# Moving two LayerNorms of an attention and mixture-of-experts kernel to other stages

## The reference, cut to what matters

```python
x1 = _layernorm(x + attn(x, x, x, causal), ln1)            # L0 self-attention
x2 = _layernorm(x1 + attn(x1, ctx, ctx), ln2)              # L0 cross-attention
x3 = _layernorm(x2 + moe(x2), ln3)                         # 8 experts, top 2, gelu
# L1: pre-norm cross-attention and MLP
q  = layer_norm(x3, l1_ln1)
kv = layer_norm(ctx, l1_ln1)                               # the context's LayerNorm
x4 = x3 + attn(q, kv, kv)
out = x4 + gelu(layer_norm(x4, l1_ln2) @ w1 + b1) @ w2 + b2   # l1_ln2: the last closing LayerNorm
```

## Time and profile before

| what | value |
|---|---|
| median of three runs | 1596.96 us (1593.52 to 1598.0) |
| profiled execution, its own time | 1599.19 us |
| its span | 1597.5 us |
| busy time, PE / DVE / ACT / POOL | 1262.5 (79%) / 961.3 (60%) / 988.5 (62%) / 916.6 us (57%) |
| mean TensorE clock granted | 0.885 of full speed |
| HBM traffic | 95.45 MB read, 50.86 MB written, 92 GB/s |
| `at_` stage, about | 0 to 580 us |
| router | 580 to 685 us |
| expert tiles | 685 to 960 us |
| combine | 961 to 1172 us |
| second block's attention | 1172 to 1472 us |
| final MLP | 1472 to 1597 us |

### The profile page before, as it was taken

The page is one execution under the profiler, slowest core; times in us unless marked ns, Lnnn a source line. Parts: engine busy times, 40 slices in busy tenths (PEclk is TensorE's granted clock), DMA queues, the critical chain, the costliest instruction groups (busy, mean ns, idle before and its releaser), DMA issues. The chain is left out here.

```text
span 1597.5 us, 60681 instructions
## 1 busy us (share of the span) xinstructions
PE 1262.5 (79%) x23128; PEld 1057.0 (66%) x23128; DVE 961.3 (60%) x2185; ACT 988.5 (62%) x2032; POOL 916.6 (57%) x1424
## 2 busy tenths in 40 slices
PE   4999999999999843879999990212149999993998
PEld 2778787778878743779999990111127787872676
DVE  4777777778787605945555553666537788881001
ACT  2778787778888600956666661545437788882333
POOL 2466675666767510079999866777324676662111
PEclk9999999999999955889999995555559999997999
DMA  3223333233332134012222223565422233322343
GB/s 100 89 88 99 96 92 103 85 94 105 92 105 89 52 122 129 0 47 70 67 68 69 67 61 103 154 171 157 128 87 87 86 99 104 106 62 62 91 118 93
DMA packets 169852, 147.65 MB, mean 92 GB/s; under 512 B 19104, under 2 KB 132256, under 8 KB 169760
## 3 DMA queue, kind: packets, MB, share of 16 engines
q1 hardware_dynamic: 161312, 129.11, 26.7%
q0 software_dynamic: 8448, 17.32, 4.6%
HBM read 95.45 MB, written 50.86 MB: 92 GB/s over the span
## 5 line engine op out<-in xcount | busy, mean ns | idle before, releaser
L741 DVE TENSOR_REDUCE at_mx<-at_ps_s 128x16 f32<-128x1024 f32 x128 | 156.0, 1219 | 107.7 <-PE at_ps_s L490 61.0
L678 ACT ACTIVATE at_pt<-at_ps_t 128x1024 f32<-128x1024 f32 x128 | 130.6, 1020 | 54.5 <-PE at_ps_t L504 53.8
L1338 POOL DMA_INDIRECT ex_xg<-x,ex_ti x136 | 148.1, 1089 | 23.3 <-issue 21.7
L671 ACT ACTIVATE at_pr<-at_dd 128x1024 f32<-128x1024 f32 x128 | 135.1, 1056 | 35.2 <-DVE at_dd L749 35.2
L1398 ACT ACTIVATE ex_hg<-ex_ps_h,ex_wt 128x128 f32<-128x128 f32 x544 | 154.8, 374 | 1.2 <-PE ex_ps_y L1367 1.2
L749 DVE TENSOR_TENSOR at_dd<-at_ps_s,at_mx 128x1024 f32<-128x1024 f32 x128 | 153.5, 1201 | 0.1
L1548 POOL DMA_INDIRECT cb_yg<-rows,cb_sl x128 | 124.9, 976 | 46.5 <-issue 44.9
L1419 DVE COPY ex_wt<-experts 128x1156 f32 x136 | 104.8, 772 | 75.4 <-DVE ex_y L1425 72.9
L1358 PE MATMUL ex_ps_h<-ex_xt,ex_wt 128*128 128x128 f32 x1088 | 147.6, 279 | 0.0
L504 PE MATMUL at_ps_t<-ident,at_pr 128*128 128x128 f32 x1024 | 140.2, 280 | 5.0 <-issue 3.1
L1367 PE MATMUL ex_ps_y<-ex_wt,ex_hg 128*128 128x128 f32 x1088 | 143.8, 275 | 0.3 <-ACT ex_hg L1398 0.3
(11 more groups left out here) (236 smaller groups left out, 3310.5 us busy)
## 6 DMA issues: line engine op xcount, KB each, us to landing
rows<-ex_y SPq DMA_DIRECT2D x136, 64.0 KB
x<-at_ln_out SPq DMA_DIRECT2D x32, 256.0 KB, 3.1
at_kx<-in_xt SPq DMA_DIRECT2D x16, 256.0 KB, 2.8
at_qx<-in_xt SPq DMA_DIRECT2D x16, 256.0 KB, 2.8
at_vin<-in_xt SPq DMA_DIRECT2D x16, 256.0 KB, 2.8
at_xr<-in_x SPq DMA_DIRECT2D x16, 256.0 KB, 3.1
x1t<-at_xt SPq DMA_DIRECT2D x16, 256.0 KB, 3.2
at_kx<-in_ctxt SPq DMA_DIRECT2D x16, 256.0 KB, 2.8
```

The lines of the kernel that those rows point to most:

```text
L671: act.activation(pr[:, p], dd[:, p], ACT.Exp, scale=SCALE).then_inc(p_ready, 1)
L678: act.activation(pt[:, 2 * h + p], ps_t[:, :, :, :], ACT.Copy).then_inc(pt_ready, 1)
L741: dve.tensor_reduce(mx[:, p], ps_s[:, :, 4 * p:4 * p + 4, :], AX.X, ALU.max).then_inc(mx_ready, 1)
L1338: pool.indirect_dma_start(out=xg[:, s, :], out_offset=None, in_=x_src, in_offset=bass.IndirectOffsetOnAxis(ap=ti[:, s:s + 1], axis=0)).the ...
```

## The change

Two LayerNorms change stage.

- **The context's.** It leaves `combine_phase` (12 statistics per group become 8, one ScalarE scaling of 4 tiles, 4 transposes and one ScalarE copy go, with a load and a store). It enters `expert_phase`, one group of 512 context tokens in each pass of 8 expert tiles. The load is issued by SyncE at tile 2 of pass q, VectorE takes statistics at tiles 4 and 5 (`context_statistics`). GpSimd computes the root (`context_root`) after its gather of tile 1 of pass q+2. VectorE scales at tile 1 of pass q+1 (`scale_context`), TensorE transposes at tile 2, VectorE copies at tile 3 (`copy_context`), and SyncE stores at tile 5. To free a PSUM bank for the transpose, `ex_ps_h` goes from four buffers to two, so `up` of tile i+2 now waits for gelu of tile i. `over_tiles` unrolls two passes at its start instead of one.
- **The last closing one.** The attention stage `l1_` no longer computes it (`closing` is false when the layer stores y), and `x4t` is gone. `mlp_phase` loads x4 three groups ahead, takes statistics on VectorE, the root on GpSimd, scales on ScalarE between its gelus, transposes on TensorE and copies on VectorE. Gain and shift are folded once into `w1g` and `b1s`.

```diff
 def attention_phase(nc, c, tag, layers):
+    closing = not layers[0].store_y
...
-                    if beyond(g, 1):
+                    if closing and beyond(g, 1):
                         pe.wait_ge(vx_ready, g + 1)
                         turn_x(a.shift(-2))
...
-                        if beyond(g, 1):
+                        if closing and beyond(g, 1):
                             pe.wait_ge(xt_ready, g - 1)
                         else:
-                            pe.wait_ge(vx_ready, 2)
+                            pe.wait_ge(vx_ready, g + 1)
                         project_out(a.shift(-1))
...
-                    if a.shift(-2).exists():
+                    if closing and a.shift(-2).exists():
                         ln.pool_rstd(pool, a.shift(-2))
...
 def mlp_phase
                 def step(g, u, k, first, last):          # TensorE
                     for f in range(FC):
                         if f < FC - 1:
-                            up(g, u, k, f + 1)
+                            up(g, u, f + 1)
                         elif not last:
-                            up(g + 1, 1 - u, k if u == 0 else k + 1, 0)
+                            up(g + 1, 1 - u, 0)
                         down(g, u, k, f)
-                up(0, 0, 0, 0)
-                over_groups(pe, step)
+                        if f == 0 and not last:
+                            turn(g + 1, 1 - u)
+                pe.wait_ge(ld, 48)
+                for f in range(FC):
+                    mm = pe.matmul(ps_b[:, f:f + 1], w1[:, P * f:P * f + P], c.col["l1_ln2_b"][:, 0:1], start=True,
+                                   stop=True)
+                mm.then_inc(fold_ready, 1)
+                turn(0, 0)
+                pe.wait_ge(w1_ready, 1)
+                up(0, 0, 0)
+                over_groups(pe, step, 1, 2)
...
+                    for f in range(3):                   # ScalarE
+                        gelu(g, f)
+                    if ahead:
+                        scale(g + 2, u, 0, 2)
+                    gelu(g, 3)
+                    if ahead:
+                        scale(g + 2, u, 2, 4)
...
+                def step(g, u, k, first, last):          # VectorE
+                    if before(g, NG - 2):
+                        moments(g + 2, u, k + 2)
+                    if not first:
+                        add(g - 1, 1 - u, k - 1 + u)
+                    if not last:
+                        copy_z(g + 1, 1 - u)
+                moments(0, 0, 1)
+                moments(1, 1, 1)
+                dve.wait_ge(fold_ready, 1)
+                dve.tensor_tensor(b1s[:, :], b1[:, :], ps_b[:, :], ALU.add)
+                dve.tensor_scalar(w1g[:, :], w1[:, :], c.col["l1_ln2_g"][:, 0:1], None, ALU.mult).then_inc(w1_ready, 1)
+                copy_z(0, 0)
...
-def expert_phase(nc, c, r, tag, x_src, out_rows):
+def expert_phase(nc, c, r, tag, x_src, out_rows, ctx_src, ct_out):
...
-        ps_h = [n.ps(f"ps_h{i}", [P, FC, P]) for i in range(HB)]
+        ps_h = [n.ps(f"ps_h{i}", [P, FC, P]) for i in range(2)]
+        ps_c = n.ps("ps_c", [P, GT])
...
+                def context_root(q):
+                    pool.wait_ge(cmv_ready, q + 1)
+                    pool.tensor_tensor(cvar[:, :], cmv[:, :, 1], c.eps[:, 0:GP], ALU.add).then_inc(cvar_ready, 1)
+                    pool.wait_ge(cvar_ready, q + 1)
+                    pool.tensor_tensor(crstd[:, :], cvar[:, :], c.minus_half[:, 0:GP], ALU.pow).then_inc(crstd_ready, 1)
+
+                def with_context(i, s, q, first, last):
+                    step(i, s, q, first, last)
+                    if s == 1 and beyond(q, 1):
+                        context_root(q - 2)
                 copy_number(0, 0)
-                over_tiles(pool, step)
+                over_tiles(pool, with_context)
+                context_root(NG - 1)
...
-                    if beyond(i, HB - 1):
-                        pe.wait_ge(hg_ready, i - HB + 1)
+                    if beyond(i, 1):
+                        pe.wait_ge(hg_ready, i - 1)
...
                     down(i, s)
+                    if s == 2 and not first:
+                        turn_context(q - 1)
...
+                def context_statistics(q, half):
+                    if half == 0:
+                        dve.wait_ge(in_c, 16 * q + 16)
+                    for t in (2 * half, 2 * half + 1):
+                        ins = dve.bn_stats(cstats[:, t, :], cx[:, t, :])
+                    if half == 0:
+                        return
+                    ins.then_inc(cstats_ready, 1)
+                    dve.wait_ge(cstats_ready, q + 1)
+                    dve.memset(ctick[:, :], 0.0)
+                    for t in range(GP):
+                        ins = dve.bn_aggr(cmv[:, t, :], cstats[:, t, :])
+                    ins.then_inc(cmv_ready, 1)
+
+                def scale_context(q):
+                    dve.wait_ge(crstd_ready, q + 1)
+                    for t in range(GP):
+                        ins = dve.tensor_scalar(zc[:, t, :], cx[:, t, :], cmv[:, t, 0:1], crstd[:, t:t + 1],
+                                                ALU.subtract, ALU.mult)
+                    ins.then_inc(zc_ready, 1)
...
                     if inside(s, last, 3):
                         weights(i + 3, (s + 3) % TU)
+                    if s == 1 and not first:
+                        scale_context(q - 1)
+                    if s == 3 and not first:
+                        copy_context(q - 1)
+                    if s in (4, 5) and not last:
+                        context_statistics(q, s - 4)
...
 def combine_phase                                        # ScalarE
-                    if not first and before(g, NG + 1):
-                        act.wait_ge(in_c[1 - u], 16 * (kp + 1))
-                        if beyond(g, 2):
-                            act.wait_ge(tc_ready, g - 2)
-                        scale(zc[:, 1 - u], cx[:, 1 - u], 1 - u, CTX).then_inc(zc_ready, 1)
```

More of the change, by code:

```diff
@@ new lines, in gelu @@
+                def gelu(g, f):
+                    m = g * FC + f
+                    act.wait_ge(h_ready, m + 1)
+                    if beyond(m, 1):
+                        act.wait_ge(used, m - 1)
+                    act.activation(hid[:, f % 2, :], ps_h[f % 2][:, :], ACT.Gelu,
+                                   bias=b1s[:, f:f + 1]).then_inc(hid_ready, 1)
+                def step(g, u, k, first, last):
+                    ahead = before(g, NG - 2)
+                    for f in range(3):
[5 more added lines that the diff above has]
+                        scale(g + 2, u, 2, 4)
@@ L1274, in mlp_phase, with step @@
+                def step(g, u, k, first, last):
+                    if before(g, NG - 2):
+                        root(g + 2, u)
+                    if not last:
+                        add_bias(g + 1, 1 - u, k + u + 1)
+                root(0, 0)
+                root(1, 1)
+                add_bias(0, 0, 1)
+                over_groups(pool, step, 1, 2)
         n.clear()
 def over_tiles(eng, step):
-    for s in range(TU):
-        step(s, s, 0, True, False)
-    with eng.Fori(1, NT // TU - 1) as q:
+    for q in range(2):
+        for s in range(TU):
+            step(q * TU + s, s, q, q == 0, False)
@@ L1283, in over_tiles @@
+    with eng.Fori(2, NT // TU - 1) as q:
         for s in range(TU):
@@ L1316, in _, with load_context, store_context @@
             def _(sp):
+                def load_context(q):
+                    if beyond(q, 0):
+                        sp.wait_ge(zc_ready, q)
+                    sp.dma_start(cx[:, :, :], ctx_src.rearrange("(g t p) d -> g p t d", t=GP, p=P)[
+                        bass.ds(q, 1)].rearrange("o p t d -> p (o t) d")).then_inc(in_c, 16)
+                def store_context(q):
+                    sp.wait_ge(zct_ready, q + 1)
+                    sp.dma_start(ct_out[:, bass.ts(q, GT)], zct[:, :]).then_inc(zc_stored, 16)
                 def step(i, s, q, first, last):
+                    if s == 2 and not last:
+                        load_context(q)
+                    if s == 5 and not first:
+                        store_context(q - 1)
                     sp.wait_ge(y_ready, i + 1)
@@ L1320, in _ @@
                 over_tiles(sp, step)
+                sp.wait_ge(zc_stored, 16 * NG)
                 for s in range(TU):
@@ L1369, in down, with turn_context @@
                     mm.then_inc(down_ready, 1)
+                def turn_context(q):
+                    pe.wait_ge(zc_ready, q + 1)
+                    for t in range(GP):
+                        tr = pe.transpose(ps_c[:, P * t:P * t + P], zc[:, t, :], c.ident[:, :])
+                    tr.then_inc(tc_ready, 1)
                 def step(i, s, q, first, last):
@@ L1588, in step @@
                         tr.then_inc(t4_ready, 1)
-                    if not first and before(g, NG + 1):
-                        pe.wait_ge(zc_ready, g)
-                        if beyond(g, 2):
```

(6 more changed lines are left out.)

281 lines of the change are left out of this document (173 added, 108 removed).

## The result

The changed kernel takes 1610.56 us in the median of four runs (1609.36 to 1612.61), the kernel before 1597.48 us in the same comparison: a ratio of 1.0086, with a 95% interval of 1.0063 to 1.0109, or +13 us. The profiled execution took 1612.61 us with a span of 1610.9 us, 13.4 us more than before.

A forecast was written before the change was run, and what follows sets the result against it. TensorE and VectorE's weights copies, with GpSimd tied to them, bound the expert stage; gathers pace combine. Sum: 31 - 4 - 7.4 - 6.0 + 7.4 = +21 us, 1620 us (1618 on the median's level), range 1609 to 1627.

The forecast's parts named there:

- Expert stage, +31 forecast: Expert stage: added transposes, VectorE insertions and waits for the root cost +31 us, bounds 7.8 to 38.
- Every insertion between a copy and the next `ex_y` delays the next copy by its length less 0.28 us.: Expert stage, VectorE: only 0.28 us is covered, the next `up` delayed equally; a pass without waits loses 1.14 us.
- A wait of 0.9 to 1.4 us in each pass.: Expert stage: VectorE's scaling waits for GpSimd's root in each pass, taken as 1.0 us; a pass loses 1.95 us.
- Rival A: Expert stage: GpSimd's root is in time, no VectorE waits after pass 1; whole +8 us, 1605; chance 0.19 including some B.
- Rival B: Expert stage: the pow blocks weights copies, up to 14.7 us above Rival A, 1605 to 1619; chance split with forecast.
- Rival C: Expert stage: weights copy off the path, insertions fit VectorE's idle time; stage +7.8, whole -2 us, 1595; chance 0.11.
- Rival E: Expert stage: two buffers make TensorE wait for gelu in each tile, 14 us more, up to 1632; chance 0.03.
- the two buffers "at nothing": Expert stage: two `ex_ps_h` buffers in place of four cost nothing, as gelu ends 0.28 us before `up`.
- Combine, -4 forecast: Combine: last steps' chain shortens by 3.4 us, last gathers land 0.6 us earlier; sum -4, bounds 0 and -12.
- rival D: Combine: weights copy off the path and gathers' pace quickens, 0.5 us a round, 8 us; time 1587; chance 0.09.
- Second attention, -7.4 forecast: Second attention: 14 groups lose 0.49 us of transposes, -6.9 us, and relieved other engines give -0.5 us.
- Boundary, -6.0 forecast: Between attention and MLP: MLP starts 9.4 us earlier, its first `up` comes 3.4 us later after start; net -6.0 us.

The follow-up runs named there:

- padded kernels: Kernel before with two or four extra VectorE operations in step 1 of each pass, which nobody waits for: 1.0018 and 1.0028 of before.
- e8_after: The changed kernel itself, unaltered, compared again with the kernel before: 1.0079 of before.
- e3_root: Changed kernel with the context's root three gathers earlier in GpSimd's queue, behind tile 6: 1.0078 of before.
- e7_root7: Changed kernel with the context's root two gathers earlier in GpSimd's queue, behind tile 7: 1.0068 of before.
- e10_noroot: Changed kernel without the context's root, scaling by the variance instead: 1.0017 of before, +2.7 us.
- e11_closing: Kernel before with only the closing LayerNorm's move, repeated on another chip: 0.9996 of before.
- e5_pad2: Kernel before with two extra 128x128 VectorE operations in step 1 of each pass, which nobody waits for: 1.0018 of before, +2.9 us.
- e6_pad4: Kernel before with four extra 128x128 VectorE operations in step 1 of each pass, which nobody waits for: 1.0028 of before, +4.5 us.
- e1_closing: Kernel before with only the closing LayerNorm's move (attention and MLP of the kernel after), first comparison: 0.9953 of before.

## Why the prediction was right in direction and where its steps were off

The forecast was +21 us (1620 on the profiled level), the measurement +13 us, inside the forecast's own range but near its lower edge. Direction and stage were right. So was the mechanism, a GpSimd queue tied to VectorE's copies and a root that comes too late, except that it strikes in half of the passes. The largest term was too large by some 9 us. Part of the agreement is luck: combine came out 2.7 us better than forecast, attention and boundary together 5.8 us worse, and inside the expert stage errors of both signs cancel.

- **Expert stage, +31 forecast, +22 measured.** Two terms of it were mis-sized. The sign "gaps on TensorE before `ex_ps_h` released by `ex_wt`" came true in small: 0.20 to 0.36 us in 14 passes, behind the statistics. The gaps after a wait for the root end on `ex_zc` and `ex_xt`.
  - *"Every insertion between a copy and the next `ex_y` delays the next copy by its length less 0.28 us."* The cover is larger. The 0.56 us between `ex_y` and the copy was taken as fixed. It shrinks as `ex_y` gets later, down to 0.14 us, and 0.28 + 0.42 = 0.70 us would be covered. The two padded kernels show 0.48 (0.60 less 0.12) and 0.78 us (1.11 less 0.33). A pass without the wait costs 0.65 us and not 1.14. If the transposes cost the 0.49 us of the forecast, 0.16 are left for VectorE's work; in the MLP, where TensorE has no gaps either, the same four cost 0.43. A second error went the other way: the four scalings take 1.12 us, taken as 0.6 and outside the bounds of 0.5 to 0.87.
  - *"A wait of 0.9 to 1.4 us in each pass."* The wait is 1.2 us, but in every second pass (8 of 16). The forecast had GpSimd tied to one gather for each copy. The trace after shows it tied except just after a wait, where it makes several gathers 1.48 us apart (802.74, 804.22, 805.70) and gains enough for one pass. So the passes 2 to 15 cost 1.2 us on average, not 1.95: 14 x 0.73 = 10 us of the error. Another 2.4 us are the second pass, 0.65 us in place of 3.1. There the forecast's 2.3 us of waiting did come true in `e8_after` (2.26 us, a pass of 17.97), and was hidden in the profiled run by its late start. The half clock and the late third `up` at the stage's start, and 0.9 us at its end, bring back 3.5 us, which the sum did not have.
- **Rival A, the root in time.** It holds in every second pass. The thought behind it, that 13.1 us of own work fit in a pass of 15.2, fails: `e3_root` and `e7_root7` put the root earlier and gained nothing that can be told, and without the root the stage lost 8.3 us of its 18.5. GpSimd makes use of its spare time only where VectorE isn't copying.
- **Rival B, the root blocks a weights copy.** It doesn't. The copies' mean went from 772 to 783 ns, 1.5 us over the stage, and the long ones, up to 1.00 us, start beside the end of a gather and not beside a pow. The kernel before has eleven of 0.86 us at such places, and `e10_noroot`, which has no root, has two of 1.00. The Trainium skill ("SBUF — State Buffer", Who interferes with whom) lets whichever of the two engines starts first block the other for its whole instruction. The trace agrees where the copy is first (a root addition of 0.75 us at 798.26, beside the copy from 798.20, against 0.20 for such an addition in the MLP). For the reverse it differs. This copy starts 0.44 us into a pow and takes its usual 0.76 us, while the pow takes 1.24 in place of 1.04:

```profile
960.12 1.24 POOL L1499 TENSOR_TENSOR ex_crstd<-ex_cvar,minus_half 128x4 f32<-128x4 f32 x1
...
960.56 0.76 DVE L1592 COPY ex_wt<-experts 128x1156 f32 x1 [0.56 <-DVE ex_y L1598]
```

  In `e3_root` a copy that starts 0.02 us behind a pow of 1.04 us takes 0.79. Spans on GpSimd are rough, but the copy's length isn't that of a blocked one.
- **Rival C, the copy isn't on the path.** Refuted by the padded kernels: work that nobody waits for costs 0.12 and 0.33 us a pass. It was nearer than its 0.11 suggested: with 16 x 0.49 = 7.8 us for the transposes, VectorE's insertions without the root cost 2.4 of the 10.2 us. This is an estimate, for no run had the transposes alone.
- **Rival E and the two buffers "at nothing".** Right in the steady stage. The start was not looked at: a wait of 0.7 us there.
- **Combine, -4 forecast, -6.7 measured.** The LayerNorm steps of the end gave 3.2 us (3.4 forecast), the earlier landing of the last gathers 3.4 (0.6 forecast) in this pair of traces. The 6.1 us of before are high, though: `e11_closing` has 4.7 with the same combine, so 1.4 us of it are that one trace's, and the earlier landing is worth 2.0. Gathers stay 1.25 us apart and take 178.5 us together in both kernels, and rival D falls.
- **Second attention, -7.4 forecast, -3.8 measured.** A group takes 15.45 us in place of 15.69: 0.24 us gained of 0.49. TensorE reaches the multiplication of `l_ot` earlier, and there a new wait stands that the kernel before doesn't have (PEld L561, 0.3 us, 11 times):

```profile
PEld l_ps_g L561 <- DVE l_ot L776: 2.9, 11, 0.3
```

  The addition `l_ot` stands behind VectorE's reduction `l_mx`, which waits for scores that TensorE computes ahead of the removed transposes. It didn't move with them.
- **Boundary, -6.0 forecast, -3.8 measured.** The store of y now ends the attention stage, as forecast. The MLP's first instruction follows it by 6.2 us (5.6 before), the load lands 4.1 us after its issue (3.1 forecast), and the whole way from the first instruction to `up` takes 10.95 us in place of the 9.4 forecast.
- **MLP, +7.4 forecast, +7.0 measured.** 0.43 us a group (7.44 us in place of 7.01).

## What to carry to other kernels

When work is put into a queue that paces itself on another engine, its spare time in the profile may not be there to be used. Its price here was the lead that it used up. Three places in that queue cost the same within the measurement, and only less work in it helped. Before costing an insertion at its length less the visible idle time, look whether other idle time on that engine is there only because the engine arrives early. And time that a moved step leaves behind must be looked for at the next wait: here half of each removed transpose group came back as one.

## What the runs showed of the hardware

- VectorE's idle time between `ex_y` and the weights copy, whose address comes from a loaded register, is 0.46 to 0.58 us in the kernel before. It was 0.32 us where `ex_y` came 0.3 us later than its input allowed (`e5_pad2`) and 0.14 us where it came 0.6 us or more later (`e6_pad4`, all 16 passes; the kernel after).
- Four VectorE operations 128x128 with two scalars for each partition take 1.12 us, their starts 0.26 us apart.
- GpSimd's small tick lasted 0.72 us at 801.73, beside a weights copy, and 0.18 us at 803.75, beside the copy from PSUM. Between 700 and 970 us all 57 ticks that no weights copy overlaps take 0.18 us, and those that one overlaps take up to 0.81. That is how its gathers can come to follow the weights copies.
- A pow of 1.04 us on GpSimd doesn't lengthen a weights copy on VectorE that starts during it: 0.76 us at 960.56 in the kernel after, 0.79 us at 709.11 in `e3_root`.
- One chip ran combine's gathers in 195 to 207 us in place of 179. In `e1_closing` its GpSimd waited for VectorE's sums 25.7 us in five places, longest 6.6 us, where the kernel after has no such wait. What held the sums isn't shown. Ratios from that chip had intervals about twice as wide.
